# Queries projected transposed, two chunks at a time, in an AdaLN block with linear attention and routed experts

## The reference, cut to what matters

```python
q = heads(h @ wq.T); k = heads(h @ wk.T); v = heads(h @ wv.T)     # 16 heads of 64
def phi(t): return exp(einsum('bhnd,md->bhnm', t, omega) - 0.5 * sum(t * t, -1)) / sqrt(64)
kv_cumsum = cumsum(einsum('bhnm,bhnd->bhnmd', phi(k), v), axis=2)
out = einsum('bhnm,bhnmd->bhnd', phi(q), kv_cumsum)
z = 1 / (einsum('bhnm,bhnm->bhn', phi(q), cumsum(phi(k), axis=2)) + 1e-6)
x = x + ga * ((out * z) merged over heads @ wo.T + bo)
# then: norm, router (softmax, top 2 of 8, capacity), experts 128 -> 512 -> 128, x + gb * result
```

## Time and profile before

| | us |
|---|---|
| median of three runs | 727.89 |
| the runs | 727.14 to 730.52 |
| the profiled execution's own time | 727.18 |
| its span, first to last instruction | 725.1 |
| granted TensorE clock over the span | 0.992 of full |

### The profile page before, as it was taken

The page is one execution under the profiler, slowest core; times in us unless marked ns, Lnnn a source line. Parts: engine busy times, 40 slices in busy tenths (PEclk is TensorE's granted clock), DMA queues, the critical chain, the costliest instruction groups (busy, mean ns, idle before and its releaser), DMA issues. The chain is left out here.

```text
span 725.1 us, 27349 instructions
## 1 busy us (share of the span) xinstructions
PE 697.4 (96%) x11452; PEld 604.1 (83%) x11452; DVE 536.0 (74%) x1685; ACT 387.6 (53%) x740; POOL 335.6 (46%) x625
## 2 busy tenths in 40 slices
PE   8999999999999999999999999999999789999956
PEld 8788888888888888888888888888887779999942
DVE  6687888878878887888878878888775456565416
ACT  5755566665656665666656566665552144544310
POOL 3002545555544445454545554545447306556550
PEclk9999999999999999999999999999999999999989
DMA  9974000000000000000000000000000154553128
GB/s 252 362 268 178 11 9 11 10 9 11 14 15 10 11 10 11 10 10 11 9 11 11 14 14 9 11 11 11 10 11 14 49 177 130 168 173 113 51 82 304
DMA packets 32705, 47.25 MB, mean 65 GB/s; under 512 B 4132, under 2 KB 20168, under 8 KB 32584
## 3 DMA queue, kind: packets, MB, share of 16 engines
q1 hardware_dynamic: 23296, 32.62, 13.4%
q0 software_dynamic: 4096, 8.42, 3.6%
q10 hardware_dynamic: 5192, 4.47, 1.9%
HBM read 22.21 MB, written 23.36 MB: 63 GB/s over the span
## 5 line engine op out<-in xcount | busy, mean ns | idle before, releaser
L1297 POOL DMA_INDIRECT y_rows<-y_sb,row_id x64 | 62.8, 982 | 66.0 <-DVE y_sb L1442 49.9
L1108 POOL DMA_INDIRECT dispatched<-h_cur,slot x64 | 67.3, 1051 | 17.8 <-issue 16.1
L1376 ACT ACTIVATE hidden<-bank,b_col 128x512 f32<-128x512 f32 x64 | 43.3, 689 | 58.2 <-PE bank L1348 57.8
L632 ACT ACTIVATE phi_k<-expo_k 128x1024 f32<-128x1024 f32 x32 | 33.9, 1058 | 74.5 <-DVE expo_k L768 70.7
L648 ACT COPY v_sb<-bank 128x512 f32<-128x512 f32 x64 | 37.6, 587 | 62.1 <-PE bank L279 58.7
L527 PEld LDWEIGHTS bank<-woT,attT 128*128 128x128 f32 x512 | 61.9, 192 | 3.2 <-ACT attT L738 0.6
L859 DVE TENSOR_TENSOR scores<-bank,within 128x512 f32<-128x512 f32 x64 | 41.2, 686 | 31.2 <-PE bank L310 31.2
L527 PE MATMUL bank<-woT,attT 128*128 128x128 f32 x512 | 62.4, 275 | 0.4 <-ACT attT L738 0.4
L1317 PE MATMUL bank<-w_sb,hidden 128*128 128x128 f32 x512 | 59.7, 275 | 0.8 <-issue 0.8
L137 POOL TENSOR_TENSOR rs<-var,power 128x1 f32<-128x1 f32 x64 | 37.1, 579 | 49.8 <-DVE var L132 49.5
L1317 PEld LDWEIGHTS bank<-w_sb,hidden 128*128 128x128 f32 x512 | 58.3, 192 | 1.2 <-issue 1.2
(11 more groups left out here) (243 smaller groups left out, 2037.9 us busy)
## 6 DMA issues: line engine op xcount, KB each, us to landing
dispatched<-blank SPq DMA_DIRECT2D x16, 524.0 KB, 3.1
region<-dispatched SPq DMA_DIRECT2D x30, 262.0 KB, 2.9
y_rows<-blank SPq DMA_DIRECT2D x8, 512.0 KB, 3.9
w_nat<-in_L_ffn_w_dram SPq DMA_DIRECT2D x8, 256.0 KB, 3.7
y_got<-y_rows SPq DMA_DIRECT2D x8, 256.0 KB, 6.8
y_got<-y_rows ACTq DMA_DIRECT2D x8, 256.0 KB, 7.4
out_dram<-x_sb SPq DMA_DIRECT2D x8, 256.0 KB, 3.7
w_sb<-in_L_ffn_w_dram ACTq DMA_DIRECT2D x6, 256.0 KB, 2.8
```

What stands on the lines that cost most here:

```text
L1108: pool.indirect_dma_start(out=dispatched[:, :], in_=h2_cur[par][:], in_offset=None, out_offset=bass.IndirectOffsetOnAxis(ap=slot[par][:, k ...
L1297: pool.indirect_dma_start(out=y_rows[:, :], out_offset=bass.IndirectOffsetOnAxis(ap=row_id[par][:, t:t + 1].bitcast(U32), axis=0), in_=y_s ...
L1376: act.activation(hidden[par][:, k, :], psum[2 + k][:], ACT.Gelu, bias=b1_col[:, bass.ds(e * KH + k, 1)]).then_inc(sem(f"hid{k}_out"), 1)
```

## The change

Queries are no longer projected as [tokens, features] but transposed, [features, tokens], so that phi_q comes out in the layout that the scores need. One step projects half of the heads for two chunks: `project_qT(n)` covers chunks of the pair n // 2 and the heads of half n % 2, with wq as the stationary operand and 2 x 128 tokens as the moving one. ScalarE copies the result to `qT`, VectorE squares it, and `exponent_qT` makes the exponents on TensorE: omega times qT, and a matrix of -0.5 times the squares, both in 64x64 tiles that add up in PSUM. ScalarE takes the exponential straight from PSUM into `phiT_q`. The weights pq, the squares, sums and exponents of q on VectorE and the transposes of phi_q go; the factor 1/8 of phi_q moves into `FEATURE_SCALE`.

The projections q, k, v, pk stand next to each other, on banks 0 to 3 instead of 0 and 1. attend(1) moves ahead of state_gain(0), the projections of pk no longer stand before add_heads, attended_T is split around the router's logits. h is prepared four chunks ahead instead of two, in three buffers of two chunks; v has three buffers. GpSimd's scatter moves ahead of the second norm's rstd. The opening prepares four chunks of h and the queries of two chunks.

The diff, cut to its core:

```diff
-    FEATURE_SCALE = float(M) ** -0.5
+    FEATURE_SCALE = 1.0 / M
-                TURNS = {0: ["q0", "k0", "v0", "pq0", "pk0"], 1: ["q1", "k1", "v1", "pq1", "pk1"],
-                         2: ["tk0", "tk1", "a0", "attT0"], 3: ["tq0", "tq1", "a1", "attT1", "rank"],
+                TURNS = {0: ["q0", "v0", "pq0"], 1: ["q1", "v1", "pq1"],
+                         2: ["tk0", "k0", "pk0", "a0", "attT0"], 3: ["tk1", "k1", "pk1", "a1", "attT1", "rank"],
+                        def project_qT(n):
+                            first = 2 * (n % 2)
+                            pair = n // 2
+                            hi, lo = h_hi[pair % 3][:, :, 0, :], h_lo[pair % 3][:, :, 0:P]
+                            pe.wait_ge(sem("h_split"), 2 * pair + 2)
...
+                            for side in range(2):
...
+                                    pe.wait_ge(sem(f"pq{side}_out"), 1 if n == 2 else n)
+                                for i in range(2):
+                                    o = q_bank(side, n)[:, i * 2 * P:(i + 1) * 2 * P].rearrange("p (c t) -> p c t", t=P)
+                                    cols = slice(side * 512 + (first + i) * P, side * 512 + (first + i + 1) * P)
+                                    pe.matmul(o, wT_hi["q"][:, cols], hi, start=True, stop=False)
+                                    pe.matmul(o, wT_lo["q"][:, cols], hi, start=False, stop=False)
+                                    mm = pe.matmul(o, wT_hi["q"][:, cols], lo, start=False, stop=True)
+                                mm.then_inc(sem(f"q{side}_in"), 1)
+                        def exponent_qT(n, c):
...
+                            pe.wait_ge(sem("q_squared"), n + 1)
+                            for i in range(2):
+                                for w, of in ((omT, qT), (minus_half, qT_square)):
+                                    for side in range(2):
+                                        for r in range(2):
+                                            cols = slice(side * 512 + i * 2 * P, side * 512 + (i + 1) * 2 * P)
+                                            mm = pe.matmul(q_bank(r, n)[half_rows(side), i * 2 * P:(i + 1) * 2 * P],
+                                                           w[half_rows(r), :], of[half_rows(r), cols],
+                                                           start=(w is omT), stop=(w is minus_half), skip_group_check=True)
 # TensorE, one step
+                            features_T(0, c, par)
+                            features_T(1, c, par)
+                            if live(c, 4):
...
+                                pe.transpose(psum[BANK["hT"]][:, 0:P], xn[par][:], ident[:]).then_inc(sem("hT_in"), 1)
+                            if live(c, 2):
+                                project_qT(c + 2)
                             if front:
-                                pe.wait_ge(sem("h_split"), c + 2)
-                                project("q0", c, nxt)
-                                project("q1", c, nxt)
-                            features_T("tq0", c, par)
-                            features_T("tk0", c, par)
...
+                                project("k0", c)
+                                project("k1", c)
+                                project("v0", c)
+                                project("v1", c)
+                                project("pk0", c)
+                                project("pk1", c)
                             if tail:
                                 attend_state(1, c - 1, nxt, (j - 1) % CPB)
+                                attend(1, c - 1, nxt, (j - 1) % CPB)
                             state_gain(0, c, par, j)
-                            if tail:
-                                attend(1, c - 1, nxt, (j - 1) % CPB)
...
                             score(0, c, par)
                             score(1, c, par)
+                            if live(c, 2):
+                                exponent_qT(c + 2, c)
                             if last:
                                 routing_T(c, par)
...
-                                project("pq0", c, nxt)
-                                project("pq1", c, nxt)
+                            if tail:
+                                attended_T(0, c)
                             if last:
                                 routing_logits(c)
                             if tail:
-                                attended_T(0, c)
                                 attended_T(1, c)
                             attend_state(0, c, par, j)
                             state_gain(1, c, par, j)
                             attend(0, c, par, j)
                             if last:
                                 routing_rank(c)
-                            if front:
-                                project("pk0", c, nxt)
-                                project("pk1", c, nxt)
                             if tail:
                                 add_heads(c)
 # ScalarE
+                        def qT_out(n):
+                            act.wait_ge(sem("pq1_in"), n)
+                            for side in range(2):
+                                act.wait_ge(sem(f"q{side}_in"), n + 1)
+                                act.copy(qT[:, side * 512:(side + 1) * 512], q_bank(side, n)[:]).then_inc(sem(f"q{side}_out"), 1)
+                        def exps_q(n):
+                            pairs = phiT_q[n // 2 % 2][:, n % 2 * 4:n % 2 * 4 + 4, :].rearrange("p (s r) t -> p r s t", r=2)
+                            for r in range(2):
+                                act.wait_ge(sem(f"pq{r}_in"), n + 1)
+                                act.activation(pairs[:, r], q_bank(r, n)[:].rearrange("p (s t) -> p s t", t=2 * P),
+                                               ACT.Exp).then_inc(sem(f"pq{r}_out"), 1)
 # VectorE
+                        def square_q(n):
+                            dve.wait_ge(sem("q1_out"), n + 1)
+                            dve.tensor_tensor(qT_square[:], qT[:], qT[:], ALU.mult).then_inc(sem("q_squared"), 1)
 # VectorE, one step
+                            if live(c, 5):
+                                first_moments(dve, c + 5)
+                            if live(c, 2):
+                                square_q(c + 2)
                             if front:
-                                sum_squares("q", c)
...
+                                sum_squares(c)
+                                exponent(0, c)
+                                exponent(1, c)
                             if tail:
                                 normalise(1, c - 1)
                             if back:
+                                state_add(0)
                                 mask(0)
                                 mask(1)
...
 # GpSimd, one step
                                 pool.tensor_tensor(x2_now[:], xs, upd[1][:], ALU.add).then_inc(sem("x2_ready"), 1)
+                                if last:
+                                    scatter()
                                 rstd(pool, "ln2", var2, rs2, c)
```

More of the change, by code:

```diff
@@ new lines, in project, with features_T @@
+                            pe.matmul(bank[:], hi_of(n)[:, toks], wT_lo[w][:, cols], start=False, stop=False)
+                            pe.matmul(bank[:], lo_of(n)[:, toks], wT_hi[w][:, cols], start=False, stop=True).then_inc(sem(kind + "_in"), 1)
+                        def features_T(half, c, par):
+                            if half and c >= 3:
+                                pe.wait_ge(sem("rank_out"), c - 2)
+                            elif c >= 2:
+                                pe.wait_ge(sem(f"attT{half}_out"), c - 1)
+                            elif c == 1:
+                                pe.wait_ge(sem(f"a{half}_out"), 1)
+                            pe.wait_ge(sem("phi_k_ready"), c + 1)
@@ L710, in rows_out, with heads_out @@
                                 act.copy(h2T[:], psum[BANK["h2T"]][:, 0:P]).then_inc(sem("h2T_out"), 1)
+                            def heads_out():
+                                for half in range(2):
+                                    act.wait_ge(sem(f"attT{half}_in"), c)
+                                    act.copy(attT[:, half * 4:half * 4 + 4, :].rearrange("p a b -> p (a b)"),
+                                             psum[BANK[f"attT{half}"]][:]).then_inc(sem(f"attT{half}_out"), 1)
                             def logits_out():
```

426 lines of the change are left out of this document (212 added, 214 removed), and 2 rows, old and new, of the table TURNS.

## The result

The changed kernel takes 763.18 us as a median of four runs (760.87 to 767.36) against 727.51 for the kernel before on the same chip: slower, ratio 1.049, 95% interval 1.043 to 1.055. The prediction was 718.7, in a range of 700 to 731.

A forecast was written before the change was run, and what follows sets the result against it. TensorE bounds the kernel: per step -3.81 removed, -0.30 joins, +3.24 added give 15.86 us, plus 0.45 wait 16.31. 29 steps -12.2, step 30 -3.7, opening +5.1, last step +1.6 sum to -9.2: 718.7 us, range 700 to 731.

The forecast's parts named there:

- up to step 1: Opening and first step: loop starts 7.8 us later, first step falls from 14.09 to 11.4; net +5.1, bounds +3 and +7.
- steps 1 to 30: Chunk loop: 29 steps at -0.42 us each, -12.2, and step 30 at -3.7.
- last step and what follows: Last step, 31: TensorE meets h2 late because the scatters move ahead of the second norm; +1.6 us.
- four tiles run together at 256 columns: exponent_qT: rival, chance 0.08, denied this; two tiles at a time add 1.74 us a step, 772 us, slower.
- a weight load lies under a half-wide matmul: project_qT: rival, chance 0.06, denied this; load and matmul in turn, 1.27 us a step more, 757 us, slower.
- The chain over ScalarE and VectorE: Projections block: rival, chance 0.16; k's squares, reduction and exponents end late; 1.0 us longer gives 730 us, no change.
- the joins: TensorE's passages between parts of a step: 0.50 us saved, some put back by the new order, net 0.30 less.
- the new wait: Head sum waits for gain1_out, no longer covered by pk: 0.45 us a step on average, bounds 0 and 0.6.
- the scores' own exit: Scores in the loop step: they lose an entry and an exit of their own, 0.14 us off.
- Step 30: Loop step with no queries left: 3.24 us less work, -3.7 us in the sum.
- The walk over the waits that stay covered: One step walked by durations: other waits stay covered, with a smallest margin of 0.6 us.
- The opening's tail: Opening, second chunk's queries: qT's single buffer makes a serial tail of 4.1 us with nothing beside it.

The follow-up runs named there:

- own_bank: Changed kernel with the head sum written to bank 0 instead of bank 7, so that it no longer waits for gain1_out: 746.15 us, ratio 1.026.
- before_adjacent: Kernel before with only attend(1) moved directly behind attend_state(1), state_gain(0) behind both: 732.89 us, ratio 1.008.
- before_block: Kernel before with its v projections moved ahead of attend_state(1) and a third buffer for v: 735.30 us, ratio 1.0098.
- v_between: Changed kernel with both v projections moved between state_gain(0) and the scores: 765.03 us, ratio 1.054.
- combined_v1_between: The combined kernel with one of the two v projections moved between attend(1) and the scores: 728.48 us, ratio 1.0014.
- gain_between: Changed kernel with attend(1) put back behind state_gain(0): 753.58 us, ratio 1.036.
- exponent_first: Changed kernel with only exponent_qT moved ahead of the scores: 767.50 us, ratio 1.053.
- opening run: Changed kernel with own buffers for the second chunk's queries and squares at the start, their copies ahead of the gates' copies: 753.93 us, ratio 1.037.
- scatter_after: Changed kernel with GpSimd's two scatters put back behind h2, as in the kernel before: 756.20 us, ratio 1.040.
- combined kernel: Changed kernel with the edits of own_bank, gain_between, scatter_after and the opening run together: 729.74 us, ratio 1.0033.
- combined_split: The combined kernel with half of exponent_qT ahead of the scores and half behind them: 723.00 us, ratio 0.9945.

## Why the prediction was wrong, point by point

| stretch | predicted | measured |
|---|---|---|
| up to step 1 | +5.1 | +9.7 |
| steps 1 to 30 | -15.9 | +15.4 |
| last step and what follows | +1.6 | +9.3 |
| sum | -9.2 | +34.4 |

**Right.** TensorE bounds the loop. project_qT was said to cost 1.50 and costs 1.52; exponent_qT 1.74, and costs 1.73 plus an exit. So two rivals fell in the timeline alone: four tiles run together at 256 columns, and a weight load lies under a half-wide matmul. On the second the Trainium skill ("TensorE: Matmul & The Clock Gate", Part 3, The mechanism) has loads overlap only where the row group differs; twelve matmuls of 128 rows with a load each in 1.52 us disagree with that. k and v got cheaper by being adjacent, to 1.39 and 1.36. The chain over ScalarE and VectorE was in time: no entry of the loop's waits names expo_k.

**The step that failed: the joins and the new wait, where the step was said to be 0.42 shorter.** A step without a gap is 16.92 to 16.99 instead of 16.31. Of the terms, four were missing or too small:
- attend(1) directly behind attend_state(1) was listed among the change's edits and priced nowhere. 0.27 a step, in the timelines of both kernels.
- The head sum's wait was right in place, cause and frequency. I took 0.45, and the gap is 0.64: both additions, and 0.14 from the end of the second to the first matmul, which I had left out. own_bank gives 17 us back, 14 of them in the loop.
- Exits into 128x128 transposes: the head sum costs 0.16 and exponent_qT 0.14 more before them. The first I had not priced. The second I had taken off as the scores' own exit; it did not go, it moved to exponent_qT.
- state_gain(0), 0.57 to 0.63 in the changed kernel, is 0.47 where attend(1) stands between it and the scores. I had no term for that.

Beyond the sum these come to some 0.9 a step (the second counts with 0.19), more than the 0.61 to 0.68 found, because the sum also missed a gain. Its prices were read in a step of 16.54 us (399.24 to 415.78) and set against a mean of 16.73. The difference is the dearer pair of state_gain(0) and attend(1) in the common step, told under before_adjacent; it went with the change. Why that pair is dearer was not traced.

Step 30 was said to be 3.7 us shorter and is 1.5 shorter (15.25 against 16.72). There attT0 waits 1.0 us for the masked scores (`PE bank L464 <- DVE scores L946`): without queries, exponent_qT is not there to cover the masks. The walk over the waits that stay covered was made for a full step only.

**The term that was not there: gaps in the instruction supply.** Steps 2 to 29 take 17.32 us on average by their starts (67.97 and 552.93), 0.33 to 0.40 more than a step without a gap. The prediction treated long 64x64 blocks as a pure gain, because they save joins. before_block has this loss without the new work; v_between takes it away at the scores and at exponent_qT, and combined_v1_between all but 0.4 us of it.

**The ends.** The opening's tail was seen and its idle time about right. What I left out is the granted clock of 0.62 behind it, until 38.60. It does not always follow such a wait: own_bank, gain_between and exponent_first have the same 2.57 idle us and a granted clock of 1.00 in the 4.42 us behind. A gap of 1.6 us at L424 near the end of step 0, again with issue as releaser, adds to it; the forecast of 11.4 us for that step compares with 14.64, and with 12.65 in the opening run. In the last step h2 is 2.5 us later, for which I had 1.6; of the 7 us that scatter_after gives back, some 4 are not the wait itself but come behind it. The largest part of the +9.3 is the tail of the experts, +4.9, which no part of the prediction looked at and no experiment explains. It takes 32.5 to 34.9 us in the profiles of the changed kernel and its eleven variants, 29.6 to 30.7 in the three of the kernel before and its variants.

So the rival of a slower kernel that came closest by number, loads not covered at 757, was wrong by mechanism. What happened is the sum of small terms that I had put at zero, in steps and at both ends. That they are the cause of most of it is shown by the combined kernel: with four of them undone, and the new way of projecting queries kept, 33.4 of 35.7 us are back. It is not so stretch by stretch: the loop is 5.3 us shorter than in the kernel before, the opening 5.0 longer, about the forecast 5.1, and the end 3.7 longer. And the idea itself was worth what the sum had said, once the order fits it: combined_split has full steps of 15.83, where I had 15.86 as work without a wait. That the two meet so closely is luck: the 0.30 of exits that the sum left out is about made up for by the 0.2 that it missed in the old step and the 0.20 that the split order saves.

**Open.** Why the gaps appear in some steps and not in others; how many instructions TensorE has at hand; what shortens the step of combined_split; why the tail of the experts is longer; and what decides whether the clock falls behind the opening's wait. That TensorE waits for instructions rests on the time from packet to restart, the same in every gap read, and on the tests with block length, not on a direct view.

## What to carry to other kernels

When an edit brings parts together that used to be apart, price every new neighbour: what the second needs finished of the first, which bank they share with another engine, and which tile size follows. Here 0.27 and 0.64 us a step, each too small to look at, gave 10 and 17 us when they were undone, 7 and 14 of them in the loop; 0.16 a step is some 5 us by estimate. An exit or an entry that one part loses may only move to its neighbour. Prices read in one step should add up to the mean that they are set against. Long runs of small matmuls save joins but can bring gaps that show "issue" as releaser; a large matmul group in the middle took most of them away, and cost as much as it gave. Idle time of TensorE at the ends of a kernel can cost more than itself when the granted clock falls around it, as it did in the last step here. And when a kernel gets slower, compare the stretches that the change does not touch as well.

## What the runs showed of the hardware

- TensorE stops for up to 1.8 us at a time, mostly inside blocks of 160 to 192 matmuls of 64x64 with a weight load each, 7 to 12 us a run between 60 and 543 us (3.7 in exponent_first, where TensorE waits elsewhere in every step). With blocks of 96 and 64 the kernel before has one such stop of 0.8, v_between 2.0 in all. In all ten stops of the changed kernel and all eight of before_block TensorE goes on 2.2 to 2.9 us after the start of a packet on the instruction queue.
- 32 matmuls of 64x64 that wait by semaphore for the 32 just issued, onto which they accumulate, start about 0.27 us late (0.52 becomes 0.79). No run parts the semaphore from the accumulation.
- Sixteen 128x128 matmuls take 1.70 us with a projection behind them and 1.86 with transposes; 32 of 64x64 with 256 columns take 1.73 before 64x64 work and 1.87 before a 128x128 transpose.
- After 2.57 us without work TensorE's granted clock was 0.62 over 4.4 us in the changed kernel and 1.00 in own_bank. Around a wait of 4.15 us it was 0.50 for 6.8 us, from 1.6 us before the wait ended.
